# List walk of a graph kernel: which step DVE's 0/1 rows signal to PE, and for which bank they wait

## The chip, the cores and the metric

One core of one Trainium2 chip. The metric is the device time of one launch in microseconds (us), the median of the runs. PE is TensorE, DVE is VectorE, ACT is ScalarE, POOL is GpSimd, SP is SyncE, which here only starts DMAs.

## The reference

Four graph layers on 3125 nodes with 256 features and 53125 directed edges (src, dst), each layer followed by a residual and a layernorm:

```python
x = layernorm(x + L0(x, edge_attr, src, dst))   # edge MLP, mean over the edges of a src node
x = layernorm(x + L1(x, edges))                 # two gcn_conv: sum of h[src] * norm over dst
x = layernorm(x + L2(x, edges))                 # three sage_conv: mean of x[src] over dst
x = layernorm(x + L3(x, edges))                 # mean of h[dst] over src
```

## The kernel before, in words

The kernel first runs the edge MLP of L0 and writes for each edge a message row to memory, sorted by bucket. A bucket is one of 125 pairs: 25 groups of source nodes (a) by 5 blocks of destination nodes (b). Layers L1 to L3 don't gather edges: they multiply by a dense table of edge counts, 3200 by 3200, that is built once. The stage that builds it, and sums the messages of L0 on the way, is the list walk; the change lies there.

**The walk** (line 1007 on) takes NST = 544 steps of 128 edges. A bucket is a block of 3 to 5 successive steps; the last block is padded with empty steps, some 50 of them. Each step:

- SP loads its 128 message rows (L1043) into one of RS = 16 places. Load u + 16 waits until step u has left its place (s_step). Ahead of the seventeenth load SP starts two loads of weights (L1054, L1055).
- DVE makes two matrices of zeros and ones from two columns of the rows. at_dst (L1087, on_dst) is 128 x 640: which destination in the block each edge has. at_src (L1095, on_src) is 128 x 128: which source. Both have HOTS = 8 places; on_dst(u) waits for the row's DMA and until step u - 8 is done. on_src(u) waits until the bank that step u adds to has been cleared (semaphore s_turns), makes at_src(u) and signals step u to PE (s_hot).
- PE waits for s_hot >= u + 1 and adds four matmuls into the step's bank: two of at_src by at_dst (L1136: the counts), and one fp32 matmul of at_src by the message rows, which the trace lists as two (L1139: the sums); it signals s_step.

Blocks take two sets of PSUM banks in turn. When PE has done a block's last step, ACT copies the counts out (L1270, cells), after the last two blocks of a group the sums too (L1274, L1276), clears the bank (L1278), signals s_turns and stores the counts. So a block's first step waits for the clearing of the block two before. Between the banks ACT and POOL work off the residual and layernorm of the group before (weigh, spread, normed, scaled on ACT).

The number of clearings that a step waits for is data: DVE reads it from turn_words, one word for four steps. DVE and PE run the walk as a loop of LOADS = 32 steps a body; at each body's start DVE does on_dst for AHEAD = 2 steps and loads eight words into registers, and PE loads two words (step_bits: which bank set each step takes). In between, and in all the rest, the order within each engine is as written.

Behind the walk PE goes straight on with the row sums of the first gcn_conv (ahead, sum_rows, L977).

Of the kernel before, what the change touches and what calls it, by code (L numbers as in the profile page):

```python
# [8 lines left out]
F32R = mybir.dt.float32r  # L9
# [3 lines left out]
ALU = mybir.AluOpType  # L13
ACT = mybir.ActivationFunctionType

P = 128
# [3 lines left out]
D = 256  # L20
# [21 lines left out]
BK = T * B  # L42
RW = D + 4
NST = 544
NH = NST // 2
RS = 16
# [42 lines left out]
def build(nc, xT, x, src_col, dst_col, edge_T, W0, b0, W1, b1, W2b, Wg, gW, gb1, gb2, sW, bl, W3, b3, out):  # L89
    ctx = ExitStack()  # L90
    with ctx:
# [29 lines left out]
        first_key = T_buf[:, BW:BW + NST]  # L121
        iota = T_buf[:, 0:BW]
        step_row = T_buf[0:1, BW + NST:BW + 2 * NST].bitcast(I32)
        step_bits = T_buf[0:1, BW + 2 * NST:BW + 2 * NST + NST // BITS].bitcast(I32)
        turn_words = T_buf[0:1, BW + 3 * NST - NST // 4:BW + 3 * NST].bitcast(I32)
        ends = T_buf[0:1, BW + 3 * NST:BW + 3 * NST + 8 * T].bitcast(I32).rearrange("p (a b) -> p a b", b=8)

        with ExitStack() as ec:
# [3 lines left out]
            def esem(name):  # L132
                return sem(name, ec)
# [429 lines left out]
            s_hot, s_rank, s_took, s_next, s_place = (esem(n) for n in ("s_hot", "s_rank", "s_took", "s_next", "s_place"))  # L563
# [436 lines left out]
        with ExitStack() as pc:  # L1000
            def psb(name, shape, dt=F32):
                return sb(name, shape, dt, pc)
# [1 line left out]
            def psem(name):  # L1004
                return sem(name, pc)

            HOTS, LOADS, AHEAD = 8, 32, 2
            rows = R_buf[:, 0:RS * RW].rearrange("p (u c) -> p u c", u=RS)
            w_raw = R_buf[:, RS * RW:RS * RW + 4 * KD * D].rearrange("p (q k n) -> p q k n", q=2, k=KD)
            at_src = psb("at_src", [P, HOTS, P])  # L1010
# [10 lines left out]
            floor, inverse, error, shift = (psb(n, [P, 2, 1]) for n in ("floor", "inverse", "error", "shift"))  # L1021
            minus_one, two = psb("minus_one", [P, 1]), psb("two", [P, 1])
            most = psb("most", [P, 4])
            cells = psb("cells", [P, 2, BW])
            s_row = [psem(f"s_row{u}") for u in range(RS)]
            s_none, s_hot, s_step = (psem(n) for n in ("s_none", "s_hot", "s_step"))
# [36 lines left out]
            @block.vector  # L1063
            def _(v):
                v.memset(none_b[:], 0.0).then_inc(s_none, 1)
                v.memset(none[:], 0.0).then_inc(s_none, 1)
                v.memset(minus_one[:], -1.0).then_inc(s_none, 1)
                v.memset(two[:], 2.0).then_inc(s_none, 1)
                v.tensor_copy(iota_h[:], iota[:]).then_inc(s_none, 1)
                ch = Chain(v, s_deg)  # L1070
                ch.link(v.tensor_scalar(dinv[:], degree[:], 1.0, None, ALU.add))
                v.tensor_scalar(dinv[:], dinv[:], 1.0, None, ALU.max).then_inc(s_sq, 1)
                v.tensor_reduce(most[:, 0:1], degree[:], mybir.AxisListType.X, ALU.max).then_inc(s_most, 1)
                ch.link(v.tensor_scalar(inv_dst[:], degree[:], 1.0, None, ALU.max))
                ch.note(v.reciprocal(inv_dst[:], inv_dst[:]))
                v.wait_ge(s_sq, 2)
                ch.note(v.reciprocal(dinv[:], dinv[:]))
                v.wait_ge(s_turned, 1)
                ch.link(v.tensor_reduce(most[0:1, 1:2], psum[5][0:1, 0:P], mybir.AxisListType.X, ALU.max))
                ch.link(v.tensor_scalar(most[0:1, 2:3], most[0:1, 1:2], float(EXACT), None, ALU.is_gt))  # L1080
                v.tensor_copy(many[:], most[0:1, 2:3]).then_inc(s_most, 1)

                def on_dst(it, u, first):

                    v.wait_ge(s_row[u % RS], 16 * (it * (LOADS // RS) + (u // RS + 1)))
                    wait(v, s_step, it * LOADS + (u - HOTS + 1) if not (first and u < HOTS) else 0)
                    v.tensor_scalar(at_dst[:, u % HOTS], iota_h[:], rows[:, u % RS, D + 2:D + 3], None, ALU.is_equal)  # L1087

                def on_src(it, u, words):

                    before = words[u // 4] >> 6
                    if u % 4:
                        before = before + ((words[u // 4] >> (6 - 2 * (u % 4))) & 3)
                    v.wait_ge(s_turns, before + 1)
                    v.tensor_scalar(at_src[:, u % HOTS].bitcast(F32R), iota[:, 0:P],  # L1095
                                    first_key[:, bass.ds(it * LOADS + u, 1)], rows[:, u % RS, D + 1:D + 2],
                                    ALU.add, ALU.is_equal).then_inc(s_hot, 1)

                def body(it, first):

                    for u in range(AHEAD):
                        on_dst(it, u, first)
                    _, words = nc.values_load_multi_w_load_instructions(
                        turn_words[0:1, bass.ds(it * (LOADS // 4), LOADS // 4)], engines=[v.engine], min_val=0,
                        max_val=64 * BK, skip_runtime_bounds_check_because="turns before a step and up to three more")
                    for u in range(LOADS):
                        if u >= AHEAD:
                            on_dst(it, u, first)
                        on_src(it, u, words)
                v.wait_ge(s_none, 5)  # L1110
                body(0, True)
                with v.Fori(1, NST // LOADS) as it:
                    body(it, False)

            @block.tensor
            def _(pe):
# [205 lines left out]
        with ExitStack() as ac:  # L1322
# [10 lines left out]
            rows = [ring[:].rearrange("p s c -> p (s c)")[:, z * NP:(z + 1) * NP] for z in range(2)]  # L1333
# [595 lines left out]
```

## Time and profile before

| | us |
|---|---|
| median of 3 runs | 3169.54 |
| lowest, highest | 3168.55, 3200.93 |
| the profiled execution | 3170.52 |
| its span, first to last instruction | 3168.8 |

The profile shows one execution. Its times count from the first instruction. A busy time is the time in which an engine works on at least one instruction; idle time before a group is put down to whatever released its instructions. PEld is PE's loading of weights, which runs beside its matmuls. Rows by stretch list PE, PEld, DVE, ACT and POOL in this order, then the granted clock as a share of full speed, the DMA engines' busy share and GB/s. "issue" as a releaser means that nothing shown held the instruction back. The walk lies between 1729 and 2173 us.

### The profile page before, as it was taken

To read this page: it belongs to the slowest core of one execution; us is meant where nothing else is said; L and a number is where in the kernel's file an instruction comes from. 1 tells how busy PE (TensorE), PEld (TensorE's weight loads), DVE (VectorE), ACT (ScalarE), POOL (GpSimd) and SP (SyncE) were. 2 spreads that over 40 slices of the span, in tenths; PEclk is the share of its full clock that TensorE was granted. 3 is DMA by queue.
4 is the path that set the end of the run, shared out by engine and by line. 5 is a ranking of instruction groups with operands and counts; after the bars stand their busy time and mean duration, and the time that the engine had idled before them with its cause. 6 is when DMAs were issued, how large, how long until landed. Compare 5 with 4: busy or idle time off the path is not lost. (4 is left out here: it accounts for less than half of the span.)

```text
span 3168.8 us, 65360 instructions
## 1 busy us (share of the span) xinstructions
PE 3049.2 (96%) x17339; PEld 2431.4 (77%) x17340; DVE 2157.3 (68%) x5603; ACT 1564.7 (49%) x3155; POOL 1377.6 (43%) x1485
## 2 busy tenths in 40 slices
PE   6699999999999999999998889999999999999899
PEld 6588888888888888888886566667777888887666
DVE  8688888888888888888885777774565222245522
ACT  2366666666666666666664777771111111011354
POOL 3577777777777777777773221210001000000111
PEclk9899999999999999999999999999999999999999
DMA  5555555555555555555553888887556777778575
GB/s 171 163 165 162 164 162 165 164 164 161 164 163 164 164 164 164 162 165 164 164 164 115 265 265 276 280 277 235 166 178 202 221 221 223 223 232 262 85 121 95
DMA packets 298299, 584.82 MB, mean 185 GB/s; under 512 B 43361, under 2 KB 150842, under 8 KB 298234
## 3 DMA queue, kind: packets, MB, share of 16 engines
q1 hardware_dynamic: 180960, 280.20, 29.7%
q0 software_dynamic: 90416, 254.46, 29.0%
q10 hardware_dynamic: 26858, 49.32, 4.3%
q8 instruction: 37, 0.61, 0.1%
q14 instruction: 28, 0.23, 0.0%
HBM read 493.97 MB, written 110.32 MB: 191 GB/s over the span
## 5 line engine op out<-in xcount | busy, mean ns | idle before, releaser
L977 PE MATMUL bank<-parts,ring 128*128 128x512 f32 x2500 | 621.8, 397 | 4.5 <-DVE T_buf L1751 2.5
L977 PEld LDWEIGHTS bank<-parts,ring 128*128 128x128 f32 x2500 | 459.9, 188 | 105.7 <-issue 5.9
L622 POOL DMA_INDIRECT msgs<-rows_out,sidx x416 | 408.0, 981 | 152.0 <-issue 95.4
L615 POOL DMA_INDIRECT p_in<-p_tab,gidx x416 | 403.3, 970 | 138.7 <-issue 115.4
L615 POOL DMA_INDIRECT q_in<-q_tab,gidx x416 | 397.9, 957 | 126.8 <-issue 125.9
L677 PE MATMUL bank<-hidden1h,w1h 128*108 128x512 f32 x936 | 406.8, 435 | 3.2 <-DVE hidden2l L865 3.2
L677 PE MATMUL bank<-w2h,hidden2h 108*128 108x256 f32 x1248 | 402.2, 322 | 0.0
L678 PE MATMUL bank<-hidden1l,w1h 128*108 128x512 f32 x936 | 368.8, 394 | 0.0
L679 PE MATMUL bank<-hidden1h,w1l 128*108 128x512 f32 x936 | 367.4, 393 | 0.0
L784 ACT ACTIVATE hidden2h<-bank,b1c 108x512 fp32r<-108x512 f32 (+1 forms) x312 | 214.5, 687 | 297.2 <-PE bank L693 297.2
L679 PE MATMUL bank<-w2h,hidden2l 108*128 108x256 f32 x1248 | 351.1, 281 | 0.0
L678 PE MATMUL bank<-w2l,hidden2h 108*128 108x256 f32 x1248 | 350.8, 281 | 0.0
L1139 PE MATMUL bank<-R_buf,at_src 128*128 128x257 f32 x1088 | 334.2, 389 | 0.0
L865 DVE TENSOR_TENSOR hidden2l<-bank,hidden2h 108x512 fp32r<-108x512 f32 (+1 forms) x312 | 215.7, 691 | 116.5 <-ACT bank L787 106.2
L770 ACT ACTIVATE hidden1h<-bank 128x512 fp32r<-128x512 f32 x416 | 246.5, 593 | 55.7 <-PE bank L671 55.7
L1136 PE MATMUL bank<-at_dst,at_src 128*128 128x320 bf16 x1088 | 238.8, 301 | 36.5 <-DVE at_src L1095 31.6
L1095 DVE TENSOR_SCALAR at_src<-T_buf,R_buf 128x128 fp32r<-128x128 f32 x544 | 207.8, 382 | 88.0 <-ACT bank L1278 78.1
L796 ACT COPY R_buf<-bank 128x256 f32<-128x256 f32 x416 | 155.7, 374 | 210.5 <-PE bank L710 204.3
L671 PE MATMUL bank<-ident,R_buf 128*128 128x128 f32 x1664 | 235.5, 274 | 20.1 <-DVE R_buf L835 12.9
L677 PEld LDWEIGHTS bank<-w2h,hidden2h 108*128 108x128 f32 x1248 | 235.2, 188 | 22.2 <-DVE rows_out L904 12.7
L772 ACT ACTIVATE bank<-bank 128x512 f32<-128x512 f32 x416 | 242.1, 582 | 13.2
L710 PE MATMUL bank<-wg,eT 128*128 128x256 f32 x832 | 248.2, 379 | 0.0
(253 smaller groups left out, 5887.6 us busy)
## 6 DMA issues: line engine op xcount, KB each, us to landing
ring<-counts SPq DMA_DIRECT2D x500, 320.0 KB, 3.3
R_buf<-msgs SPq DMA_DIRECT2D x544, 130.0 KB, 3.1
counts<-cells ACTq DMA_DIRECT2D x125, 320.0 KB, 3.4
eT<-in_edge_T SPq DMA_DIRECT2D x104, 256.0 KB, 2.9
R_buf<-counts POOLq DMA_DIRECT2D x25, 480.0 KB, 5.3
R_buf<-counts POOLq DMA_DIRECT2D x25, 320.0 KB, 5.7
p_in<-p_tab,gidx POOLq DMA_INDIRECT x416, 3.2
q_in<-q_tab,gidx POOLq DMA_INDIRECT x416, 3.3
```

What stands on the lines that cost most here:

```text
L615: pool.indirect_dma_start(out=rows_in[:, z, c], out_offset=None, in_=tab[:], in_offset=bass.IndirectOffsetOnAxis(ap=gidx[:, z, which, c:c ...
L622: pool.indirect_dma_start(out=msgs[:], in_=rows_out[:, z, c], in_offset=None, out_offset=bass.IndirectOffsetOnAxis(ap=sidx[:, z, c:c + 1], ...
L671: mm = pe.transpose(bT[c % 2][:, k * C:(k + 1) * C], pre1[:, z, c, k * P:(k + 1) * P], ident[:])
L677: pe.matmul(out, lh.bitcast(F32R), rh.bitcast(F32R), start=first, stop=False)
L678: pe.matmul(out, lh.bitcast(F32R), rl.bitcast(F32R), start=False, stop=False)
L679: return pe.matmul(out, ll.bitcast(F32R), rh.bitcast(F32R), start=False, stop=last)
L710: pe.matmul(bO[c % 2][:, D:2 * D], eT[:, z, e], wg[:], start=True, stop=True).then_inc(s_L2, 1)
L770: act.activation(hidden1h[:, z, :, e].bitcast(F32R), src, ACT.Tanh).then_inc(s_hi1, 1)
L772: act.activation(src, src, ACT.Tanh).then_inc(s_th1, 1)
L977: mm = pe.matmul(bU[t].rearrange("p (w c) -> p w c", w=2), ring[:, cell(odd, a), t * P:(t + 1) * P].bitcast(dt), parts[k % 2][:, :, a].bit ...
L1136: pe.matmul(bank[:, half * 512:half * 512 + 2 * CW][:, bass.ds(at[u], NW)], at_src_b[:, u % HOTS, :, 1], at_dst[:, u % HOTS, half * NW:(ha ...
L1139: pe.matmul(bS[:, bass.ds(at[u], SW)], at_src[:, u % HOTS], rows[:, u % RS, 0:SW], start=False, stop=False, skip_group_check=True).then_in ...
```

## The change

DVE's operation for step u now waits for the bank of step u - 4 and signals step u - 4 (LEAD = 4). The first four at_src wait for no bank and signal nothing. Behind the loop DVE loads one word, and signals the last four steps by four memsets of one column (passed), each behind the wait for its step's bank. on_dst is as before, so at most eight steps have their 0/1 rows made and not yet used, and signals are at most four steps ahead of PE. The words of turn_words are read from four steps earlier; in the first body they begin at word 0. PE, ACT, SP and POOL have the same instructions as before.

```diff
--- before.py
+++ after.py
@@ -1004,7 +1004,7 @@
             def psem(name):
                 return sem(name, pc)
 
-            HOTS, LOADS, AHEAD = 8, 32, 2
+            HOTS, LOADS, AHEAD, LEAD = 8, 32, 2, 4
             rows = R_buf[:, 0:RS * RW].rearrange("p (u c) -> p u c", u=RS)
             w_raw = R_buf[:, RS * RW:RS * RW + 4 * KD * D].rearrange("p (q k n) -> p q k n", q=2, k=KD)
             at_src = psb("at_src", [P, HOTS, P])
@@ -1021,6 +1021,7 @@
             floor, inverse, error, shift = (psb(n, [P, 2, 1]) for n in ("floor", "inverse", "error", "shift"))
             minus_one, two = psb("minus_one", [P, 1]), psb("two", [P, 1])
             most = psb("most", [P, 4])
+            passed = psb("passed", [P, LEAD])
             cells = psb("cells", [P, 2, BW])
             s_row = [psem(f"s_row{u}") for u in range(RS)]
             s_none, s_hot, s_step = (psem(n) for n in ("s_none", "s_hot", "s_step"))
@@ -1086,31 +1087,48 @@
                     wait(v, s_step, it * LOADS + (u - HOTS + 1) if not (first and u < HOTS) else 0)
                     v.tensor_scalar(at_dst[:, u % HOTS], iota_h[:], rows[:, u % RS, D + 2:D + 3], None, ALU.is_equal)
 
-                def on_src(it, u, words):
-
-                    before = words[u // 4] >> 6
+                def cleared(word, u):
+
+                    before = word >> 6
                     if u % 4:
-                        before = before + ((words[u // 4] >> (6 - 2 * (u % 4))) & 3)
+                        before = before + ((word >> (6 - 2 * (u % 4))) & 3)
                     v.wait_ge(s_turns, before + 1)
-                    v.tensor_scalar(at_src[:, u % HOTS].bitcast(F32R), iota[:, 0:P],
-                                    first_key[:, bass.ds(it * LOADS + u, 1)], rows[:, u % RS, D + 1:D + 2],
-                                    ALU.add, ALU.is_equal).then_inc(s_hot, 1)
+
+                def on_src(it, u, words, first):
+
+                    ready = not (first and u < LEAD)
+                    if ready:
+                        cleared(words[(u - LEAD if first else u) // 4], u)
+                    step = v.tensor_scalar(at_src[:, u % HOTS].bitcast(F32R), iota[:, 0:P],
+                                           first_key[:, bass.ds(it * LOADS + u, 1)], rows[:, u % RS, D + 1:D + 2],
+                                           ALU.add, ALU.is_equal)
+                    if ready:
+                        step.then_inc(s_hot, 1)
+
+                def words_from(at, n):
+
+                    _, words = nc.values_load_multi_w_load_instructions(
+                        turn_words[0:1, bass.ds(at, n)], engines=[v.engine], min_val=0,
+                        max_val=64 * BK, skip_runtime_bounds_check_because="turns before a step and up to three more")
+                    return words
 
                 def body(it, first):
 
                     for u in range(AHEAD):
                         on_dst(it, u, first)
-                    _, words = nc.values_load_multi_w_load_instructions(
-                        turn_words[0:1, bass.ds(it * (LOADS // 4), LOADS // 4)], engines=[v.engine], min_val=0,
-                        max_val=64 * BK, skip_runtime_bounds_check_because="turns before a step and up to three more")
+                    words = words_from(it * (LOADS // 4) - (0 if first else LEAD // 4), LOADS // 4)
                     for u in range(LOADS):
                         if u >= AHEAD:
                             on_dst(it, u, first)
-                        on_src(it, u, words)
+                        on_src(it, u, words, first)
                 v.wait_ge(s_none, 5)
                 body(0, True)
                 with v.Fori(1, NST // LOADS) as it:
                     body(it, False)
+                words = words_from((NST - LEAD) // 4, LEAD // 4)
+                for u in range(LEAD):
+                    cleared(words[u // 4], u)
+                    v.memset(passed[:, u:u + 1], 0.0).then_inc(s_hot, 1)
 
             @block.tensor
             def _(pe):
```

## Rows read from the trace of the kernel before

**Rows 1.** Page of the kernel before, its first line.

```profile
span 3168.8 us, 65360 instructions
...
```

**Rows 2.** Busy times by stretch: us, each engine's busy (x instructions), clock, DMA.

```profile
...
1755.00:2137.00 382.00, 352.17 (x1879) 240.12 (x1878) 296.15 (x941) 296.55 (x692) 74.91 (x117) 1.00 0.88 274
2137.00:2173.00 36.00, 36.00 (x204) 26.42 (x203) 29.29 (x94) 0.31 (x2) 0.94 (x1) 1.00 0.79 236
...
```

**Rows 3.** Groups by line, 1729 to 2173 us: busy, mean ns | idle before.

```profile
...
L1136 PE MATMUL bank<-at_dst,at_src 128*128 128x320 bf16 x1088 | 238.8, 301 | 36.5 <-DVE at_src L1095 31.6 <-issue 3.5
L1087 DVE TENSOR_SCALAR at_dst<-iota_h,R_buf 128x640 bf16<-128x640 f16 x543 | 212.3, 393 | 5.1 <-DMA R_buf<-msgs 1.9 <-PE bank L1139 1.4 <-issue 1.1
L1095 DVE TENSOR_SCALAR at_src<-T_buf,R_buf 128x128 fp32r<-128x128 f32 x544 | 207.8, 382 | 88.0 <-ACT bank L1278 78.1 <-issue 8.7
...
L1270 ACT COPY cells<-bank 128x640 f32<-128x640 f32 x125 | 85.8, 686 | 129.7 <-PE bank L1139 123.0 <-DMA counts<-cells 3.3 <-issue 3.1
...
```

**Rows 4.** Waits, 1729 to 2172 us: us in total, times, longest.

```profile
...
ACT cells L1270 <- PE bank L1139: 87.3, 68, 7.0
...
```

**Rows 5.** Timeline at one bank wait: start us, us, instruction [idle <-releaser].

```profile
...
1912.84 0.69 ACT L1278 COPY bank<-none 128x640 f32<-128x640 f32 x1
...
1913.68 0.35 DVE L1095 TENSOR_SCALAR at_src<-T_buf,R_buf 128x128 fp32r<-128x128 f32 x1 [1.53 <-ACT bank L1278]
...
1914.38 0.10 PEld L1136 LDWEIGHTS bank<-at_dst,at_src 128*128 128x128 bf16 x1 [0.97 <-issue]
...
```

**Rows 6.** Timeline of DVE at the walk's start.

```profile
...
1729.44 0.65 DVE L1095 TENSOR_SCALAR at_src<-T_buf,R_buf 128x128 fp32r<-128x128 f32 x2 [0.41 <-issue]
...
1730.85 0.34 DVE L1095 TENSOR_SCALAR at_src<-T_buf,R_buf 128x128 fp32r<-128x128 f32 x1
...
1731.41 0.34 DVE L1095 TENSOR_SCALAR at_src<-T_buf,R_buf 128x128 fp32r<-128x128 f32 x1
```

**Rows 7.** Timeline of the slow stretch, and its busy times and clock.

```profile
...
1741.66 0.73 DVE L1087 TENSOR_SCALAR at_dst<-iota_h,R_buf 128x640 bf16<-128x640 f16 x1 [1.91 <-DMA R_buf<-msgs]
...
1745.05 0.51 PE L1136 MATMUL bank<-at_dst,at_src 128*128 128x320 bf16 x2 [3.50 <-DVE at_src L1095]
...
1746.56 0.69 ACT L1270 COPY cells<-bank 128x640 f32<-128x640 f32 x1 [3.73 <-PE bank L1139]
...
1747.88 0.69 ACT L1278 COPY bank<-none 128x640 f32<-128x640 f32 x1
...
1751.75 0.62 PE L1136 MATMUL bank<-at_dst,at_src 128*128 128x320 bf16 x2
...
1745.30:1752.10 6.80, 5.88 (x18) 3.40 (x17) 6.80 (x16) 2.08 (x5) 3.11 (x2) 0.50 0.78 232
...
```

**Rows 8.** Timeline of DVE at the first and the last break of 32 steps.

```profile
...
1758.74 0.33 DVE L1095 TENSOR_SCALAR at_src<-T_buf,R_buf 128x128 fp32r<-128x128 f32 x1
...
1760.07 0.75 DVE L1095 TENSOR_SCALAR at_src<-T_buf,R_buf 128x128 fp32r<-128x128 f32 x2 [0.41 <-ACT bank L1278]
...
2145.23 0.33 DVE L1095 TENSOR_SCALAR at_src<-T_buf,R_buf 128x128 fp32r<-128x128 f32 x1
...
2146.90 0.74 DVE L1095 TENSOR_SCALAR at_src<-T_buf,R_buf 128x128 fp32r<-128x128 f32 x2 [0.63 <-issue]
```

**Rows 9.** Timeline of PEld at the first break, step 128, the last.

```profile
...
1759.51 0.29 PEld L1136 LDWEIGHTS bank<-at_dst,at_src 128*128 128x128 bf16 x2
...
1761.95 0.10 PEld L1136 LDWEIGHTS bank<-at_dst,at_src 128*128 128x128 bf16 x1 [1.79 <-issue]
...
1839.32 0.32 PEld L1136 LDWEIGHTS bank<-at_dst,at_src 128*128 128x128 bf16 x2
...
1840.96 0.22 PEld L1136 LDWEIGHTS bank<-at_dst,at_src 128*128 128x128 bf16 x2 [0.97 <-issue]
...
2149.00 0.31 PEld L1136 LDWEIGHTS bank<-at_dst,at_src 128*128 128x128 bf16 x2
...
2149.91 0.10 PEld L1136 LDWEIGHTS bank<-at_dst,at_src 128*128 128x128 bf16 x1 [0.24 <-issue]
```

## The prediction

> **What bounds the kernel now.** I read the page first: the span is 3168.8 us [rows 1]. The edit touches the list walk alone, so next come the stretches of the trace. The walk lies between 1729 and 2173 us. In its middle, 1755 to 2137 us, PE is busy 352 of 382 us, ACT 297 and DVE 296; in its last 36 us PE is busy all the time; TensorE's granted clock is 1.00 in both [rows 2]. PE's matmuls follow one another without a break both through the walk and into the row sums behind it, so what PE loses in the walk moves the end, unless a wait for ACT swallows it. By line, PE's first matmul of a step (L1136) sat idle 36.5 us, 31.6 of it until at_src; DVE's at_dst and at_src take a mean of 393 and 382 ns; at_src sat idle 88.0 us, 78.1 of it until ACT had cleared a bank; and ACT's copy of a bank sat idle 129.7 us, 123.0 of it until PE [rows 3].
>
> The cycle is PE, ACT, DVE, PE. The list has 125 blocks of 3 to 5 steps, the last one padded. PE ends a block, ACT copies its bank (L1270) and clears it (L1278), DVE lets go the step two blocks on, PE walks on. At a bank wait the rows read: the clear ends at 1912.84 + 0.69 = 1913.53, at_src starts at 1913.68 and ends at 1914.03, and PE's weight load starts at 1914.38 [rows 5]. So 0.15 + 0.35 + 0.35 = 0.85 us lie between the clear and PE.
>
> PE has a pace of its own of 0.70 us a step: in the last 36 us, where nothing holds it up, it does 204 matmuls, four a step [rows 2]; DVE with its pair of operations 0.55 (1730.85 to 1731.41 is 0.56) [rows 6]. So 544 steps would take PE 383 us; it takes 443. The other 60 us are bank waits, a slow stretch at the start, and one break in every 32 steps, where both engines load registers and branch.
>
> **The change, part by part.**
>
> *The signal.* Today at_src(u) waits for the bank of step u and signals u. Afterwards at_src(u+4) waits for the bank of u and signals u. Between the clear and the signal there still stands one at_src of 0.35 us [rows 5], and the next signal still takes a further pair, at_dst and at_src, 0.55 us. The four rows that stand ready are never signalled faster than DVE makes four more. Of the 0.85 us nothing goes: 0 us. From above the gain is bounded by all of PE's idle time until at_src, 31.6 us [rows 3]; I take 0, since the same operation ends the wait.
>
> *The start.* PE's first step waits for at_src(4) instead of at_src(0): 1731.41 instead of 1729.44 is 1.97 us later [rows 6]. Then comes the slow stretch. at_dst(16) waited for its row's DMA until 1741.66, and PE idled 3.50 us until it started step 16 at 1745.05 [rows 7]. DVE's course there is set by DMA and by its slow operations, not by PE; afterwards its at_src(16) carries the signal of step 12. So PE stands four steps further back: it starts 12 at 1745.05, and 16 where it now starts 20, at 1751.75 [rows 7]. By then the clock is full again. Step 16 ends its bank's block: about 1.05 us to its end, then the copy from 1746.56 to the clear's end at 1748.57, 2.01 us as now [rows 7], gives a clear at 1754.8, and 0.85 later PE starts step 20, at 1755.7 instead of 1751.75: +4.0 us. The lower bound is the plain 1.97; the upper is 4 x 1.40 = 5.6, four steps at the low clock, 0.50 from 1745.3 to 1752.1 [rows 7].
>
> *The breaks at every 32nd step j.* DVE there does two at_dst, loads eight registers and only then at_src(j). From at_src(j-1) to at_src(j) it takes 1.33 us at the first of the 16 breaks (1758.74 to 1760.07) and 1.67 at the last (2145.23 to 2146.90) [rows 8]; the 16 average 1.84, against 0.55 elsewhere. Today this delays the signal of j, and PE has its own break before the same step: at step 128, where at_src had been ready, 1839.32 to 1840.96 is 1.64 us [rows 9]. The two breaks lie side by side. The mean of PE's 16 steps there is 1.84 too (2.44 at the first, 1759.51 to 1761.95, 0.91 at the last, 2149.00 to 2149.91 [rows 9]). Where DVE was in time, as at 128, they took about 1.67. Afterwards DVE's break delays the signal of j-4, and PE's break still stands at j: the two no longer cover each other. PE has 0.70 us of its own work under DVE's 1.84 and a lead of signals that grows by 0.15 a step from 0 after each bank wait, some 0.3 us on average. It loses 1.84 - 0.70 - 0.30 = 0.84 us at j-4 and wins back 1.84 - 1.67 = 0.17 at j: 0.67 net, times 16 is 10.7 us. A part is swallowed: at 68 of 125 banks ACT was waiting for PE and passes a delay on, at 57 it was late by itself [rows 4]. 10.7 x 68/125 = 5.8 us. Bounds: 0 if bank waits cover all of it, 16 x 0.84 = 13.4 if none and nothing is won back.
>
> *The buffers.* at_dst(u+4) still waits until step u-4 has left its place of eight. Signals can now lead PE by four steps, not eight. Outside the breaks that costs nothing: from the end of step u-4, some 1.1 us after its start, an at_dst and an at_src take 0.65, 1.75 in all, and PE wants u after 2.8. At a break two at_dst and the load stand in between, and 1.75 becomes about 2.9: the cost already counted.
>
> *The rows' DMAs.* A row must have landed four steps earlier. There are 16 places, and at_dst waited once, 1.9 us, in the whole walk [rows 3]; that once is in the start. 0 us; SP's issues move with PE's steps and pass no other queue.
>
> *The end.* One more load of a register and four memsets of one column, on a DVE that has nothing else left while PE runs without a break [rows 2]. 0 us; 0.3 at most, by an at_src's 0.35 in their place. Behind a waiting at_src stands only the next at_dst; no other engine waits for that.
>
> Sum: 4.0 + 5.8 = 9.8 us. The profiled execution took 3170.5 us around its span of 3168.8, 1 us over the median of 3169.5. On its own time 3180.3; on the median 3179.3 us.
>
> **The rivals.**
>
> *Rival A, the stalls behind DVE go.* If four ready rows do let PE run on, up to 31.6 us of idle time [rows 3] leave: 3169.5 - 31.6 = 3138 at most, half of it likelier, 3154. For it: PE does wait for at_src. Against it: the signal still costs a whole operation [rows 5].
>
> *Rival B, the breaks are hidden.* DVE's break falls into bank waits, as at the first of the 16 (idle until the clear, 0.41 us [rows 8]), and only the start stays: 3169.5 + 2 to 4, about 3172.
>
> *Rival C, nothing is swallowed.* PE is the bound in its whole row of steps: 4.0 + 13.4 = 17.4, 3187 us.
>
> *Rival D, the clock falls: slower.* PE would idle twice in each 32 steps, at j-4 and at j. After its idle 3.50 us the granted clock stood at 0.50 (1.2 of 2.4 GHz) for the 6.8 us from 1745.3 to 1752.1 [rows 7], of which half is lost, 3.4 us. Once in each break, 16 x 3.4 = 54 us and the 9.8: 3233. It decides once two idle gaps close together count like one long one. Against it: the middle 382 us hold 15 gaps of up to 1.8 us and the clock there is 1.00 [rows 2]. The Trainium skill, "TensorE: Matmul & The Clock Gate", section "A second HAM failure mode: psum-queue depth-cycling", speaks for it: short idle times between groups of matmuls, repeated often enough, made the clock swing between its levels. By that rule this walk, which cycles through banks, would have shown it already; the trace does not.
>
> **How the numbers follow.** The forecast 0.55, Rival B 0.22, Rival C 0.12, Rival A 0.07, Rival D 0.04. Predicted time: 3179 us. The range reaches from 3169 (Rival B with a fully hidden start) to 3189 (Rival C). A measurement of this kernel can tell about 1% from no change, 32 us: faster only in the upper half of Rival A, 0.03; slower in Rival D, 0.04; within 1% 0.93.
>
> **What would show it.** PE's first walk matmul some 2 us later against DVE's first at_dst; a shift of about 4 us at step 25; the span of the walk up by about 10 us; DVE's longest intervals still at every 32nd at_src, and now a PE gap of about 1.6 us between starts four steps ahead of PE's own break; idle time of PE until at_src up from 31.6, not down; busy times of at_dst and at_src unchanged. The forecast is wrong if the time from a clear's end to PE's weight load is well below 0.85 us, if no gap shows at j-4, or if the clock leaves 1.00 in the middle.

## The result, and the profile after

The changed kernel took 3215.84 us (median of 4 runs, 3211.63 to 3219.03), beside it the kernel before 3171.38 (4 runs, 3168.55 to 3200.93). The ratio on record is 1.0128, 95% interval 1.01 to 1.0157; it isn't the quotient of the two medians, which is 1.0140, here and below. So the kernel is slower by 41 us by the ratio and 44 by the medians, less than 2% and clear of the noise. The forecast was 3179 us in a range up to 3189; the measured time lies outside it.

The profiled execution took 3219.03 us. The first line of its page answers to [rows 1], whose span is 48.5 us shorter:

```profile
span 3217.3 us, 65364 instructions
...
```

By stretch (columns as in [rows 2]) the same 382 us in the walk's middle hold less work, and the granted clock is no longer 1.00. The last two rows are two short stretches in it, at half speed, 1.2 instead of 2.4 GHz:

```profile
...
1755.00:2137.00 382.00, 332.12 (x1698) 224.37 (x1696) 275.24 (x849) 268.87 (x627) 66.35 (x109) 0.96 0.80 249
...
1793.60:1797.00 3.40, 3.40 (x12) 2.39 (x10) 1.97 (x7) 0.00 (x0) 0.00 (x0) 0.50 0.32 78
1936.90:1943.70 6.80, 5.33 (x16) 3.63 (x17) 3.90 (x12) 2.19 (x5) 0.00 (x0) 0.50 0.31 101
...
```

PE got through 1698 matmuls where it did 1879. By line, over the walk (1729 to 2220 us; busy, mean ns | idle before), the rows that answer to [rows 3]:

```profile
...
L1154 PE MATMUL bank<-at_dst,at_src 128*128 128x320 bf16 x1086 | 246.7, 310 | 65.1 <-DVE at_src L1102 59.5 <-issue 4.5
L1088 DVE TENSOR_SCALAR at_dst<-iota_h,R_buf 128x640 bf16<-128x640 f16 x544 | 215.0, 397 | 26.1 <-PE bank L1157 20.2 <-issue 1.6 <-DMA R_buf<-msgs 1.1
L1102 DVE TENSOR_SCALAR at_src<-T_buf,R_buf 128x128 fp32r<-128x128 f32 x544 | 205.5, 378 | 103.6 <-ACT bank L1296 76.6 <-issue 25.4
...
L1154 PEld LDWEIGHTS bank<-at_dst,at_src 128*128 128x128 bf16 x1087 | 108.9, 100 | 179.2 <-issue 113.1
...
L1288 ACT COPY cells<-bank 128x640 f32<-128x640 f32 x124 | 85.2, 687 | 138.7 <-PE bank L1157 133.6 <-issue 4.8
...
```

PE's idle time until at_src is 59.5 us instead of 31.6, and at_src's idle time for "issue" 25.4 instead of 8.7. "issue" means that nothing in the list of instructions held it. The waits (us in total, times, longest; the first answers to [rows 4]):

```profile
...
ACT cells L1288 <- PE bank L1157: 133.6, 72, 10.4
...
PE bank L1154 <- DVE at_src L1102: 59.5, 38, 4.1
DVE at_src L1102 <- issue: 25.4, 12, 3.0
...
DVE at_dst L1088 <- PE bank L1157: 20.2, 38, 0.9
...
```

I call the time from PE's weight load for step 0 to that for step 543 the walk. It was 441.6 us and is 487.7: 46.0 of the 48.5 us. The timelines of DVE and PEld at the first break (step 32) show where they arise; they answer to [rows 8, 9]:

```profile
...
1759.51 0.33 DVE L1102 TENSOR_SCALAR at_src<-T_buf,R_buf 128x128 fp32r<-128x128 f32 x1
1759.77 0.37 DVE L1088 TENSOR_SCALAR at_dst<-iota_h,R_buf 128x640 bf16<-128x640 f16 x1
1760.43 0.39 DVE L1088 TENSOR_SCALAR at_dst<-iota_h,R_buf 128x640 bf16<-128x640 f16 x1 [0.30 <-PE bank L1157]
1763.52 0.76 DVE L1102 TENSOR_SCALAR at_src<-T_buf,R_buf 128x128 fp32r<-128x128 f32 x2 [2.70 <-issue]
...
1760.72 0.31 PEld L1154 LDWEIGHTS bank<-at_dst,at_src 128*128 128x128 bf16 x2
...
1764.22 0.22 PEld L1154 LDWEIGHTS bank<-at_dst,at_src 128*128 128x128 bf16 x2 [2.82 <-issue]
...
```

From at_src(31) to at_src(32) DVE takes 4.01 us where it took 1.33, with 2.70 us idle for "issue". PE stands still from step 27 to step 28, 3.50 us from start to start. Over the 16 breaks DVE's interval went from a mean of 1.84 to 3.62 us.

What DVE does in that idle time is a row of its sequencer, found by the source line of the load (x count, duration ns min/median/max, first and last start). First the kernel before, then the changed one:

```profile
...
L1103 DVEq TENSOR_LOAD <-T_buf x17: 594/780/1446, 1728.4 to 2146.0; - x17
...
```

```profile
...
L1110 DVEq TENSOR_LOAD <-T_buf x18: 319/2374/3024, 1728.8 to 2215.9; - x18
...
```

The load at the first break fills the idle 2.70 us: it runs from 1760.6 for 2.65 us.

```profile
...
L1110 DVEq TENSOR_LOAD <-T_buf x1: 2648/2648/2648, 1760.6 to 1760.6; - x1
...
```

The load of eight registers takes three times as long. The first body's took 0.86 us as before, the one-word load at the end 0.32, and the other 16 between 1.85 and 3.02, mean 2.40, where before their mean was 0.83. One thing about them differs: eight words were read from word 8 x it of the table, and are now read from 8 x it - 1, so that they begin one word off a place that is a multiple of eight.

On some of the chips used below the kernel before itself took 3579 to 3750 us, all of it more ahead of the walk; so runs are compared by their walk, and whole times only where the kernel before repeated within some 0.6% (those are called steady). A fall is a stretch at the lower clock that begins within the walk, the one near its start (1745.3 us before, [rows 7]) included. In most runs the clock is still low from earlier as the walk begins; the times at the lower clock hold that stretch too, the counts of falls don't.

### The profile page after: what moved, and what is told of

It is laid out like the page before. It is cut to its first block and busy times, and to the rows that moved or that the text cites. A ratio compares the mean times of both kernels' runs of the same rounds, so it can differ in the third digit from the quotient of the medians.

```text
span 3217.3 us, 65364 instructions
## 1 busy us (share of the span) xinstructions
PE 3067.5 (95%) x17338; PEld 2442.2 (76%) x17340; DVE 2169.6 (67%) x5607; ACT 1565.2 (49%) x3155; POOL 1374.2 (43%) x1485
## 5 line engine op out<-in xcount | busy, mean ns | idle before, releaser
L1157 PE MATMUL bank<-R_buf,at_src 128*128 128x257 f32 x1088 | 346.5, 401 | 0.0
L1154 PE MATMUL bank<-at_dst,at_src 128*128 128x320 bf16 x1088 | 247.2, 310 | 65.1 <-DVE at_src L1102 59.5
```

The lines of the kernel that those rows point to most:

```text
L1154: pe.matmul(bank[:, half * 512:half * 512 + 2 * CW][:, bass.ds(at[u], NW)], at_src_b[:, u % HOTS, :, 1], at_dst[:, u % HOTS, half * NW:(ha ...
L1157: pe.matmul(bS[:, bass.ds(at[u], SW)], at_src[:, u % HOTS], rows[:, u % RS, 0:SW], start=False, stop=False, skip_group_check=True).then_in ...
```

## The experiments

**1. Both kernels again (e7_before_again, e8_after_again).** No edit.

> The kernel before, unchanged, for its profile beside those of the others. The walk from PE's first weight load of step 0 to that of step 543 took 441.6 us in the first profile. If the walk does not depend on the chip, it is 441 to 444 us here too, with loads of 0.6 to 1.4 us, whatever the whole kernel takes.

> The changed kernel, unchanged. Its walk, measured the same way, took 487.7 us in the first profile. If it does not depend on the chip: 483 to 490 us, loads of 1.8 to 3.0 us, eight or more falls of the clock in the walk, and 42 to 47 us more than the kernel before in the whole.

Measured on one chip: before again 3171.22 us, ratio 0.9999 (0.999 to 1.0009), walk 443.8, one fall. Changed again 3211.89 us, ratio 1.0131 (1.0114 to 1.0148), walk 481.7, 8 falls, loads:

```profile
...
L1110 DVEq TENSOR_LOAD <-T_buf x18: 315/2190/3049, 1727.3 to 2208.4; - x18
...
```

The effect is of the kernel, not of a run. Both the walk and the whole came out a little under what was expected of them (483 to 490 and 42 to 47 us). The two traces of the same changed kernel differ by 6.0 us in the walk. The time at the lower clock in it is 47.7 and 36.2 us. An estimate: half of that difference, 5.8, is lost, and the loads (2.40 and 2.31 us) add 1.4, 7.2 in all; so half is somewhat too much. Falls look like a cost of their own, and their number isn't fixed.

**2. The table one word further (e1_aligned, e9_aligned_again, e14_aligned_third).** The changed kernel with its words in an aligned place; the ends table moves by eight to make room.

```diff
-        turn_words = T_buf[0:1, BW + 3 * NST - NST // 4:BW + 3 * NST].bitcast(I32)
+        turn_words = T_buf[0:1, BW + 3 * NST - NST // 4 + 1:BW + 3 * NST + 1].bitcast(I32)
```

> The changed kernel, with the table turn_words moved by one word, so that DVE's load of eight words in each body of 32 steps starts at a multiple of eight words again (it starts one word before one in the changed kernel). Theory 1, the address: the load took 2.40 us on average against 0.83 before because it starts one word off; here it falls back to 0.6 to 0.9 us, DVE's interval from at_src(j-1) to at_src(j) from 3.62 to about 1.9, PE's gap four steps ahead of its own break from 3.4 to about 1.6 between starts, and the granted clock stays at 1.00 behind the slow stretch. Time 3176 to 3186 us, which is the forecast on record. Theory 2, the lead: the load is long because DVE runs only four steps ahead and meets it with an empty queue; the load stays at 2.2 to 2.6 us and the time at 3210 to 3220.

> The same kernel as e1_aligned. Its walk was 452.9 us there, 5 to 11 us over that of the kernel before, on a chip where all the times before the walk were longer and scattered by 3%. Here the whole time tells too. Theory 1: load 0.6 to 0.9 us, walk 449 to 454 us, whole 8 to 12 us over the kernel before. Theory 2 (the lead): whole 40 us over it.

> The same kernel as e1_aligned, for its whole time on a chip that runs the kernel before in 3170 us. Theory 1: walk 450 to 454 us, whole 9 to 14 us over the kernel before (0.3 to 0.45%). If the part that falls away with the place of the load is smaller in the whole than in the walk, 20 us or more.

Measured: walk 452.9, 452.6 and 452.2 us, with 3, 2 and 1 falls, of which 2, 1 and 0 lie in its middle, where none was expected. Whole: 3193.51 against 3181.7 us in the third, 11.8 more by the medians, ratio 1.0024 (1.0011 to 1.0037), which is 8; on chips with scattered times 1.0139 (0.9994 to 1.0284) and 1.0079 (1.0023 to 1.0136). The third's loads, in whose count the first body's, now the unaligned one at 2.09 us, and the last one-word load stand too, and its middle by stretch:

```profile
...
L1110 DVEq TENSOR_LOAD <-T_buf x18: 321/612/2092, 1736.0 to 2188.8; - x18
...
```

```profile
...
1770.00:2187.00 417.00, 382.09 (x2032) 260.04 (x2030) 329.81 (x1017) 295.89 (x691) 73.14 (x118) 1.00 0.84 264
...
```

One word's distance takes 29 to 36 of the 38 to 46 us in the walk away, the long loads and nearly all falls with it. What is left, some 10 us in the walk, is the change itself. PE's interval is 1.70 us at j-4 and 1.72 at j in the mean, up to 2.48.

The fall in the middle of the second run stands behind two shorter intervals of PE, one after the other (steps 315 and 316; timeline of PEld, then the stretch that follows):

```profile
...
2477.26 0.22 PEld L1154 LDWEIGHTS bank<-at_dst,at_src 128*128 128x128 bf16 x2 [1.12 <-issue]
...
2479.39 0.22 PEld L1154 LDWEIGHTS bank<-at_dst,at_src 128*128 128x128 bf16 x2 [1.58 <-issue]
...
2480.10:2483.50 3.40, 3.40 (x12) 2.12 (x11) 1.39 (x5) 1.37 (x3) 0.00 (x0) 0.51 0.39 119
...
```

Start to start these intervals are 1.77 and 2.13 us. The first run has a fall at the same place, behind 1.76 and 2.13, and one behind a single 2.76 (step 252); e13_three_loads below has one behind 1.77 and 2.26. The third run has 1.79 and 2.13 there and no fall.

**3. The kernel before with its table off its place (e2_before_unaligned, e11_off_by_four).** The same line in the kernel before, by one word, and by four.

> The kernel before, with the table turn_words moved by one word, so that its load of eight words starts one word behind a multiple of eight. Theory 1, the address: the load takes 1.8 to 2.9 us in all 17 bodies; the break delays one signal, beside PE's own break, so PE's step there goes from 1.84 to about 3.2 us between starts; 16 x 1.4 = 22 us, some of it swallowed by bank waits: 3183 to 3195 us, with few falls of the clock or none. Theory 2, the lead: nothing changes, 3168 to 3174 us.

> The kernel before, with the table moved by four words (16 bytes), so that each load of eight words starts halfway between two multiples of eight. If only a start at a multiple of eight words is loaded at once, the loads take 1.8 to 2.9 us and the walk is 460 to 468 us, as in e2_before_unaligned. If a multiple of four is enough, they take 0.6 to 0.9 us and the walk 441 to 444.

```profile
...
L1103 DVEq TENSOR_LOAD <-T_buf x17: 1846/2268/2796, 2214.2 to 2657.6; - x17
...
```

```profile
...
L1103 DVEq TENSOR_LOAD <-T_buf x17: 595/665/1522, 2233.5 to 2652.6; - x17
...
```

By one word: loads of 2.33 us in the mean, DVE's break 3.30 instead of 1.84, the walk 466.2 us with 5 falls, 4 of them in its middle, where few or none were expected (whole 1.0142, 1.0032 to 1.0252, on a chip with scattered times). So 16 breaks, 1.46 us longer each, 23.3 us in all, and the falls behind them give 24.6 us more walk, in a kernel without the edit. By four words, in a single run: 443.1 us and the old loads, a median of 0.67 us. In that run a start at a multiple of four words does; one word off does not.

**4. Is it the length of the break alone? (e13_three_loads, e18_five_more).** The first had two more aligned loads in each body of the aligned kernel. Nothing used their results, and they were not in the program that ran: its trace has one load a body.

> e1_aligned with its load of eight words done three times over in each body but the first, so that a break holds three loads of 0.6 us, 1.8 us in all, on the aligned place. It parts the length of the break from the place of the words. If only the length of DVE's break counts, this comes to what the unaligned load of the changed kernel does: PE's gap at j-4 about 3 us between starts, the granted clock falling in the walk again, walk 475 to 490 us, whole 35 to 45 us over the kernel before. If the unaligned place does harm in another way too, the walk stays below 470 us.

It is a fourth run of the aligned kernel: walk 451.5 us, one fall, 3195.99 us, 14.3 more than the kernel before, ratio 1.0041 (1.0028 to 1.0054), which is 13. On its question it says nothing. A version in which words of all three loads were in use (e17_three_live) left no measurement. The second lengthens the break with work that stays:

```diff
+                    for extra in range(0 if first else 5):
+                        v.tensor_scalar(more[:, extra], iota_h[:], rows[:, 1, D + 2:D + 3], None, ALU.is_equal)
                     words = words_from(it * (LOADS // 4) - (0 if first else LEAD // 4), LOADS // 4)
```

> The aligned four-step kernel with five more operations of at_dst's form (128x640, about 0.31 us from one to the next) ahead of the load in each of the 16 loop bodies, into spare buffers that nobody reads: DVE's break is as long as the changed kernel's (about 1.55 us more), and the table's words lie in an aligned place. Length theory: only how long DVE's break is counts. The walk from the first to the last weight load goes from 452 us to 475 to 490 (the changed kernel has 482 to 488), the gap from step to step at the fourth step ahead of the break's becomes about 3.3 us, and the granted clock falls 5 times or more (1 to 3 times with the words aligned, 8 and 10 in the changed kernel). Rival: the words' place slows something else as well: then the walk stays under 470 us with at most 3 falls.

Measured: walk 463.2 us, one fall of 3.4 us in its middle, 3195.25 against 3172.01 us, ratio 1.0078 (1.0061 to 1.0094). The timeline of DVE at its first break:

```profile
...
1755.43 0.33 DVE L1103 TENSOR_SCALAR at_src<-T_buf,R_buf 128x128 fp32r<-128x128 f32 x1
...
1756.69 2.03 DVE L1121 TENSOR_SCALAR more<-iota_h,R_buf 128x640 bf16<-128x640 f16 x5
1758.64 0.59 DVE L1103 TENSOR_SCALAR at_src<-T_buf,R_buf 128x128 fp32r<-128x128 f32 x2
...
```

PE's interval at j-4 is 2.54 us. The break is longer by less than intended: its sequencer loads the words while the five operations still run, and the mean interval is 2.80 us, 0.84 more than the aligned kernel's 1.96 and not 1.55. So the expectation's numbers were for a length that the run didn't have, and the walk under 470 us doesn't decide for the rival. What it shows: 16 x 0.84 = 13.4 us more break gives 11.0 us more walk with the words in their place, although it has 6.1 us less at the lower clock than the aligned kernel's third run, by its start. Counted from step 26 on, behind the start, it is 14.0 us more, with 3.4 more at the lower clock. Length by itself costs, nearly all of it. A mean break of 3.6 us with aligned words wasn't reached, so an effect of the place beyond the length isn't excluded; nothing here needs one.

**5. One-word loads (e6_one_word).** The kernel before, its eight-word load replaced by a one-word load at every fourth step.

```diff
+                        if u % 4 == 0:
+                            _, word = nc.values_load_multi_w_load_instructions(
+                                turn_words[0:1, bass.ds(it * (LOADS // 4) + u // 4, 1)], engines=[v.engine], min_val=0,
...
+                            words += word
```

> The kernel before, with the eight words loaded one by one, each ahead of the four steps that use it. Theory 1 (a load off its place goes word by word, some 0.22 us a word behind the first 0.3): each load takes about 0.32 us; at a body's start 0.3 us instead of 0.83 leave PE's own break as the longer one, 16 x 0.17 = 3 us gained; the other 119 loads stand behind queued operations and cost nothing, or, where DVE has just come from a bank wait, part of 0.32 us. Walk 436 to 442 us. The rival: each load holds DVE up by 0.3 us every fourth step, 0.55 + 0.08 us a step, still under PE's 0.70, but the lead behind a bank wait is used up: 445 to 460 us.

```profile
...
L1108 DVEq TENSOR_LOAD <-T_buf x136: 300/363/1109, 1727.6 to 2171.6; - x136
...
```

Measured: walk 449.3 us, 5.5 more than the kernel before on the same chip, as the rival had it; 3175.26 us, ratio 1.0017 (1.0008 to 1.0027). 136 loads of 0.52 us in the mean are 70 us of DVE's sequencer instead of 14. Spread out, most of it is hidden, but not all, and it is no gain.

**6. The eight-word load at the fourth step (e4_load_at_4, e10_load_at_4_again, e15_load_at_4_third).** The changed kernel loads one word at the body's start, and the eight words, aligned, ahead of at_src(4).

```diff
-                    words = words_from(it * (LOADS // 4) - (0 if first else LEAD // 4), LOADS // 4)
+                    words = [] if first else words_from(it * (LOADS // 4) - 1, 1)
...
+                        if u == LEAD:
+                            on_dst(it, u + 1, first)
+                            words = words_from(it * (LOADS // 4), LOADS // 4)
```

> The changed kernel, with the load of eight words moved to u = 4 of the body, where it starts at a multiple of eight, and a load of one word left at the body's start. The step that it delays is then the step at which PE has its own break. Theory 1 (address and double break): the eight words take 0.6 to 0.9 us beside PE's break, the one word 0.3 us, PE's gap at j-4 falls below 1.4 us between starts and only the start of the walk (+4 us) and a small rest stay: 3173 to 3180 us, less than the first of these runs. If the four-step lead itself is what costs, it stays at the time of the first run or above.

> The same kernel as e4_load_at_4, whose walk was 447.7 us. Theory 1: walk 445 to 449 us, whole 3 to 7 us over the kernel before and some 5 us under e9_aligned_again, since the long load stands beside PE's break again.

> The same kernel as e4_load_at_4, for its whole time beside e14. Walk 447 to 449 us, whole 4 to 8 us over the kernel before: what is left of the four-step lead when the load is aligned and stands beside PE's break, almost all of it the walk's start.

Measured: walk 447.7, 447.5 and 446.5 us, with a fall or none. Whole, on the steady chip: 3187.85 us, ratio 1.0025 (1.0012 to 1.0038); on the others 0.9957 (0.9878 to 1.0037) and 1.02 (1.0108 to 1.0292), too scattered to tell. It wins 5 of the aligned kernel's 10 us in the walk: PE's interval at j-4 is 1.42 to 1.45 us instead of 1.70 to 1.75, at j 1.75 to 1.80 instead of 1.64 to 1.73. Two short breaks cost less than one long one, as the longer of them delays the signal of step j, where PE has its own break.

**7. The wait on PE instead of DVE (e3_pe_waits).** The kernel before; PE loads the words, computes the number and waits for the bank itself, DVE waits for no bank.

```diff
+                        before = turns[u // 4] >> 6
+                        if u % 4:
+                            before = before + ((turns[u // 4] >> (6 - 2 * (u % 4))) & 3)
+                        pe.wait_ge(s_turns, before + 1)
                         pe.wait_ge(s_hot, i + 1)
```

> The kernel before, but the wait for the bank stands on PE: DVE's at_src waits for no bank and signals its own step, PE loads the eight words and waits for s_turns itself. Theory 1 says that what a bank wait costs is the operation between the clear and the signal, and that ready rows help only if no operation stands between: the 0.85 us from a clear's end to PE's weight load fall to 0.2 to 0.35, at some 50 bank waits that is 25 to 30 us; the DVE operations slowed in a block cost nothing any more (8 us); PE's break grows by a load of 0.6 us, 16 times, 10 us. Time 3140 to 3160 us. The rival: PE's sequencer gets some four more instructions a step and its step becomes longer than 0.70 us; 0.05 us more a step give 27 us back, time 3165 to 3185.

Measured: walk 527.8 us, 86 more; whole 1.029 (1.0202 to 1.0379), on a chip with scattered times. Both the theory (3140 to 3160 us) and its rival (3165 to 3185) expected far less. The waits and three weight loads of steps that follow one another:

```profile
...
PEld bank L1136 <- issue: 212.5, 494, 3.0
...
DVE at_dst L1087 <- PE bank L1139: 143.9, 367, 3.2
...
```

```profile
...
2302.33 0.22 PEld L1136 LDWEIGHTS bank<-at_dst,at_src 128*128 128x128 bf16 x2 [0.46 <-issue]
...
2303.31 0.22 PEld L1136 LDWEIGHTS bank<-at_dst,at_src 128*128 128x128 bf16 x2 [0.44 <-issue]
...
2304.17 0.22 PEld L1136 LDWEIGHTS bank<-at_dst,at_src 128*128 128x128 bf16 x2 [0.31 <-issue]
...
```

Now DVE waits 143.9 us for PE, and PE for little but "issue": until at_src 11.4 us, until ACT's clear 8.3. A step takes 0.86 to 0.98 us in these rows, in the median 0.955 instead of 0.705. The trace lists the register instructions of PE's sequencer: before, 6 of them in 445 of 543 steps; here 9 in 248 steps, 8 in 125 and 7 in 102, 2.3 more in the mean. The steps with 6, 7, 8 and 9 take 0.705, 0.797, 0.884 and 0.985 us in the median here, so each costs about 0.09 us, and PE's own instruction stream is the bound. What a bank wait costs without an operation between, which was the question, this run can't tell.

**8. The signal by a memset (e5_signal_by_memset; with the lead e12_memset_and_lead, e16_memset_and_lead_again).** The idea of the change in another form: at_src is made ahead of the bank wait, and what stands behind the wait and signals is a memset of one column. One ready row instead of four.

```diff
-                    v.wait_ge(s_turns, before + 1)
                     v.tensor_scalar(at_src[:, u % HOTS].bitcast(F32R), iota[:, 0:P],
                                     first_key[:, bass.ds(it * LOADS + u, 1)], rows[:, u % RS, D + 1:D + 2],
-                                    ALU.add, ALU.is_equal).then_inc(s_hot, 1)
+                                    ALU.add, ALU.is_equal)
+                    v.wait_ge(s_turns, before + 1)
+                    v.memset(passed[:, u % HOTS:u % HOTS + 1], 0.0).then_inc(s_hot, 1)
```

> The kernel before, with at_src(u) made ahead of the wait for the bank, and a memset of one column behind the wait, which signals step u. Theory 1 (what counts is the operation between the clear and the signal): the 0.85 us from a clear's end to PE's weight load at a bank wait fall by about 0.29 us, at some 50 bank waits 14 us; DVE takes about 0.1 us more a step, 0.65 against PE's 0.70, so that its lead grows more slowly and the slowed operations and the breaks cost up to 6 us more. Walk 428 to 438 us against 441.6. The rival: DVE's step grows to 0.75 us or more, DVE becomes the bound, and the walk is 445 us or longer.

> e4_load_at_4 (four steps' rows ahead, aligned load) with the signal given by a memset behind the wait, as in e5_signal_by_memset. It tells whether four ready rows bring anything once no long operation stands between the clear and the signal. Theory 1: from a clear's end to PE's weight load 0.45 us as in e5, the walk 8 us shorter than e4's 447.7: 438 to 442 us, and slower than e5's 434.4 by the start of the walk (about 4 us) and the shorter lead, since each further signal still waits for two operations. The rival, that ready rows help by themselves: 434 us or less.

> The same kernel as e12_memset_and_lead, for its whole time beside e15. Walk 441 to 443 us, whole within 3 us of the kernel before and 6 us or more over e5_signal_by_memset, which has no lead and took 6 us less than the kernel before.

The timeline of the first at one bank wait:

```profile
...
1913.37 0.69 ACT L1280 COPY bank<-none 128x640 f32<-128x640 f32 x1
...
1914.12 0.06 DVE L1099 MEMSET passed<- 128x1 f32 x1
...
1914.51 0.22 PEld L1138 LDWEIGHTS bank<-at_dst,at_src 128*128 128x128 bf16 x2 [0.73 <-issue]
...
```

The clear ends at 1914.06 and PE's weight load starts at 1914.51: 0.45 us, the median of 46 such waits too, against 0.82 before. The walk is 434.4 us, 9.3 less than before on the same chip, although DVE's pair grew from 0.552 to 0.562 us. Whole: 3164.35 against 3170.45 us, ratio 0.9977 (0.9966 to 0.9988): it beats both kernels, by little. With the four-step lead and the load as in 6: walk 441.9 and 440.5 us, 5.6 and 6.1 less than that kernel without the memset on the same chips; whole 3185.01 us, ratio 1.0009 (0.9996 to 1.0022), and 1.0127 (1.0047 to 1.0208) on a chip with scattered times. The lead takes back what the memset gives.

## Why the prediction was wrong, point by point

**The signal: right.** Nothing was won between clear and PE. In the changed kernel (answers to [rows 5]):

```profile
...
1985.96 0.69 ACT L1296 COPY bank<-none 128x640 f32<-128x640 f32 x1
...
1986.80 0.35 DVE L1102 TENSOR_SCALAR at_src<-T_buf,R_buf 128x128 fp32r<-128x128 f32 x1 [1.48 <-ACT bank L1296]
...
1987.48 0.22 PEld L1154 LDWEIGHTS bank<-at_dst,at_src 128*128 128x128 bf16 x2 [0.87 <-issue]
...
```

1987.48 less 1986.65 is 0.83 us; the median is 0.82 in both kernels. "The same operation ends the wait" holds, and with it Rival A falls. Run 8 shows what was in it: a shorter operation behind the wait, not more rows.

**The start: right.** Measured from DVE's first at_dst, PE is 1.8 us later at step 0 (forecast 1.97) and 3.6 at steps 24 to 27 (forecast 4.0); in the second pair of runs 1.8 and 2.6.

**The breaks: the step that failed.** "DVE there does two at_dst, loads eight registers and only then at_src(j)" was priced at its old 1.84 us, moved as it stood to j-4. The diff changes the load's first word as well, from 8 x it to 8 x it - 1, and the load with it: the price was 3.62. The rest of the step was sound. Its own sum, less 0.70 and 0.30, gives a loss at j-4 of 2.62; PE's interval there went from 0.77 to 3.40, 2.63. In the aligned kernel, with a break of 1.96, the sum gives 0.96 and the trace 0.93 (0.77 to 1.70). There 0.93 - 0.12 won back at j, times 16, is 13.0 us. From step 26 on, its walk grew by 8.9 (425.1 against 416.2, means of four and two runs), with 3.4 us at the lower clock in the mean where there was none. If half of those is lost, 7.2 to 8.9 of 13.0 arrived, 0.55 to 0.69, where the forecast took 68/125 = 0.54 [rows 4]. With the start's 2.6 to 3.6 that is 10 to 12.5 us for the change as forecast, against 9.8. Whole, the two runs on the steady chip measured 11.8 and 14.3 us by the medians and 8 and 13 by the ratios, 1.2 of them by that kernel's own unaligned first load. I did cost the load's place at nothing without a word; the trace before had no unaligned load, and its bound should have been left open.

**Rival D: half right, and given too little.** The clock fell 10 times in the walk, 8 times in the other run. The argument against it was "15 gaps of up to 1.8 us" at clock 1.00. Those 1.8 are idle time ahead of a weight load; from start to start the middle before had intervals of up to 2.49 us. That speaks for gaps of that size alone. Now the gaps at j-4 are 2.61 to 4.21 us from start to start. In the profiled run each fall in the middle came behind one of 3.42 us or more, and none behind those of 2.99 or less; but gaps of 3.45 and 3.50 had none either, and in the second run one fall came behind 2.89. A second gap close by, as the rival had it, was not always needed: the fall of 1936.9 began while PE still stood in one longer gap (PE's timeline):

```profile
...
1938.38 0.71 PE L1154 MATMUL bank<-at_dst,at_src 128*128 128x320 bf16 x2 [3.27 <-DVE at_src L1102]
...
```

The Trainium skill's "TensorE: Matmul & The Clock Gate", section "A second HAM failure mode: psum-queue depth-cycling", whose rule I had weighed and set aside, names frequent short idling between groups of matmuls. The runs fit it in part: with gaps of 1.7 us in the mean at twice as many places (run 2, at j-4 and at j) the clock was 1.00 through the middle of the third run, while in three other executions of that kernel it fell behind two intervals in a row of 1.8 and 2.1 to 2.3 us, which is the rival's own condition. Long gaps brought most falls, two close together some; what decides between a fall and none at the same place no run shows.

**What the 44 us are made of, an estimate.** The start differs from run to run (25.4 to 28.4 us up to step 26), so I count from step 26 to step 543, from the traces (us; DVE's break is its mean interval from at_src(j-1) to at_src(j)):

| | step 26 to 543 | of it at the lower clock | DVE's break |
|---|---|---|---|
| before, two runs | 415.7, 416.6 | 0, 0 | 1.84, 1.88 |
| aligned, four runs | 426.1, 425.2, 423.8, 425.2 | 6.8, 3.4, 0, 3.4 | 2.00, 2.01, 1.96, 2.03 |
| aligned, five more operations | 437.8 | 3.4 | 2.80 |
| before, one word off | 439.6 | 13.7 | 3.30 |
| changed, two runs | 459.9, 453.8 | 37.5, 23.9 | 3.62, 3.53 |

Against the aligned kernel's third run, which has no fall here, the changed kernel takes 36.1 us more with 37.5 at the lower clock, and its second run 30.0 more with 23.9. If half of that time is lost, 18.8 and 12.0, the rest, 17.4 and 18.1, is the longer break, of 16 x 1.66 = 26.6 and 16 x 1.57 = 25.1 us of it. But in run 4 at least 12.3 of 13.4 us of longer break arrived; at that rate it would be 24 of the first run's 36.1, and 12 the clock. Together with the 11 to 12 of the change itself: a quarter is the lead, 40 to 55% the length of the loads, the rest the clock. How the last two share isn't settled better than this, as no run has long breaks at the full clock.

**Buffers and DMAs: right in sign.** at_dst waited 20.2 us for PE instead of 1.4 [rows 3], at places where signals stand at most four ahead and DVE has nothing to do; for a row's DMA it waited 1.1. "1.75 becomes about 2.9" at a break was short by the same load.

**The end: right.** Timelines of DVE and PEld:

```profile
...
2216.39 0.06 DVE L1131 MEMSET passed<- 128x1 f32 x1 [0.36 <-issue]
...
2216.93 0.24 DVE L1131 MEMSET passed<- 128x1 f32 x2 [0.21 <-issue]
...
2219.91 0.31 PEld L1154 LDWEIGHTS bank<-at_dst,at_src 128*128 128x128 bf16 x2
...
```

The last signal was given by 2217.17, and PE loads step 543's weights at 2219.91, without a break behind the one before.

**The chances.** Rivals B and C stood on either side of a sum that was right for an aligned load. None of the cases had a dearer operation in it: each took over from the trace what the diff had altered.

## What to carry to other kernels

An edit that shifts an index also shifts an address: when a load is moved "as it stands", compare its first word and price the new address as a new operation, with an open bound. The sequencer's rows show such a load, while the list of busy times shows only "idle until issue". Making rows ready ahead of a wait helps only if what stands behind the wait gets shorter; one ready row and a cheap signal did more than four ready rows behind a full operation. And gaps of one size that leave the clock alone say nothing of longer ones: here the intervals grew from at most 2.6 us to as much as 4.2.

## What the runs showed of the hardware that I had not expected

- A load of eight registers on DVE from a row of on-chip memory took 0.59 to 1.55 us from word 0 of eight (from word 4, in one run, 0.60 to 1.52), and 1.84 to 3.05 from one word beside such a place; a load of one word 0.30 to 1.11. The Trainium skill ("Runtime: NRT & Kernel Launch", section "Instruction fetch mechanics") gives about 200 ns per register for loads from device memory; here, from on-chip memory, the aligned load is at 75 to 190 per register, the unaligned one at 230 to 380.
- DVE's sequencer runs such a load while earlier operations are still being carried out: five more operations of 0.31 us ahead of it lengthened the break by 0.84 us only (run 4).
- PE's sequencer took about 0.09 us for each register instruction; 2.3 more in a step, in the mean, moved the bound from matmuls to instructions (run 7).
- The clock fell for 3.4 or 6.8 us at a time, mostly behind single intervals of 2.8 us and more between the weight loads of two steps, but also behind two in a row of 1.8 and 1.9 to 2.3; in one execution at one break, and in another of the same kernel at another.
